# Issuing the four rough score products of the 8-dim attentions together, ahead of the weighing and the denominators

## The reference

```python
q = (x @ Wq + bq).reshape(B, N, 16, 8)
k = (y @ Wk + bk).reshape(B, M, 16, 8)       # y is x or the context
v = (y @ Wv + bv).reshape(B, M, 16, 8)
scores = einsum('bnhd,bmhd->bhnm', q, k) * scale   # + bias table in one, causal mask in another
attn = softmax(scores, axis=-1)
out = einsum('bhnm,bmhd->bnhd', attn, v).reshape(B, N, 128)
```

## Time and profile before

| what | us |
|---|---|
| median of 3 runs (3710.57 to 3713.22) | 3712.27 |
| the profiled execution, its own time | 3711.78 |
| its span from the first to the last instruction | 3710.0 |
| PE busy | 2897.6 (78%) |
| DVE busy | 2003.4 (54%) |
| ACT busy | 1416.0 (38%) |
| POOL busy | 1365.0 (37%) |
| TensorE's mean granted clock | 0.866 of full speed |

### The profile page before, as it was taken

How to read it: one execution, slowest core, us unless ns; L and a number is a source line. 1 busy time by engine, 2 the same in 40 slices (tenths; PEclk the granted TensorE clock), 3 DMA queues, 4 the chain that set the end, 5 groups by cost and what they waited for, 6 DMA issues and landing times. The chain is left out here.

```text
span 3710.0 us, 81900 instructions
## 1 busy us (share of the span) xinstructions
PE 2897.6 (78%) x32225; PEld 2044.2 (55%) x32225; DVE 2003.4 (54%) x5288; ACT 1416.0 (38%) x3283; POOL 1365.0 (37%) x1685
## 2 busy tenths in 40 slices
PE   6961566776686997996899869964589999979978
PEld 4540333554444775664799756641156666655657
DVE  6988887044463444663444445644455555535634
ACT  3541554144344553443222135520033333335544
POOL 3430343163201113544233334535533333325555
PEclk9985676577687998996999979967789999989979
DMA  2000000200000000000000000000000000000000
GB/s 92 3 2 2 1 1 1 79 21 1 6 1 30 2 2 36 3 3 1 7 1 1 1 13 2 2 38 0 0 5 2 2 2 2 2 7 2 2 1 23
DMA packets 24441, 36.96 MB, mean 10 GB/s; under 512 B 568, under 2 KB 21184, under 8 KB 23232
## 3 DMA queue, kind: packets, MB, share of 16 engines
q1 hardware_dynamic: 24096, 32.10, 2.7%
HBM read 29.87 MB, written 2.23 MB: 9 GB/s over the span
## 5 line engine op out<-in xcount | busy, mean ns | idle before, releaser
L1190 POOL TENSOR_TENSOR L_attn__qk<-L_attn__turned 128x512 f32<-128x512 f32 x128 | 161.5, 1273 | 381.0 <-DVE L_attn__turned L1299 381.0
L4079 PE MATMUL psum<-L_ffn_hT,weights 128*128 128x256 f32 x1024 | 244.9, 383 | 11.7 <-PEq L56 11.7
L1299 DVE TENSOR_TENSOR L_attn__turned<-psum,weights 128x1024 f32<-128x1024 f32 x128 | 153.7, 1221 | 153.1 <-PE psum L1406 149.9
L774 DVE TENSOR_REDUCE L_xattn__nm<-psum 128x8 bf16<-128x1024 f32 x128 | 156.4, 1225 | 147.2 <-PE psum L967 140.7
L4079 PEld LDWEIGHTS psum<-L_ffn_hT,weights 128*128 128x128 f32 x1024 | 186.8, 192 | 32.5 <-issue 11.8
L4018 DVE TENSOR_TENSOR L_ffn__e_a<-L_ffn__e_sg,psum 128x512 f32<-128x512 f32 x128 | 88.0, 688 | 187.4 <-ACT L_ffn__e_sg L4010 187.4
L4010 ACT ACTIVATE L_ffn__e_sg<-psum 128x512 f32<-128x512 f32 x128 | 76.4, 597 | 259.6 <-PE psum L4079 259.6
L714 ACT ACTIVATE L_xattn__pT<-psum 128x1024 f32<-128x1024 f32 x128 | 124.0, 1021 | 59.4 <-PE psum L995 59.4
L4090 PEld LDWEIGHTS psum<-weights,L_ffn__e_a 128*128 128x128 f32 x1024 | 134.4, 191 | 7.3 <-DVE L_ffn__e_a L4018 0.7
L1406 PE MATMUL psum<-L_attn__xT,weights 128*128 128x256 f32 x512 | 136.8, 401 | 1.7 <-DVE L_attn__turned L1299 1.0
L4090 PE MATMUL psum<-weights,L_ffn__e_a 128*128 128x128 f32 x1024 | 135.0, 275 | 0.5 <-DVE L_ffn__e_a L4018 0.5
(11 more groups left out here) (658 smaller groups left out, 8033.9 us busy)
## 6 DMA issues: line engine op xcount, KB each, us to landing
L_xattn__toeplitz<-s4d_kernel SPq DMA_DIRECT2D x8, 1024.0 KB, 5.6
weights<-pack SPq DMA_DIRECT2D x1, 3328.0 KB, 10.8
weights<-pack SPq DMA_DIRECT2D x1, 3140.0 KB, 11.4
weights<-pack SPq DMA_DIRECT2D x1, 2370.0 KB, 9.1
out_dram<-X SPq DMA_DIRECT2D x1, 2048.0 KB, 8.7
weights<-pack SPq DMA_DIRECT2D x1, 1732.5 KB, 10.3
ctxT<-ctxT_in SPq DMA_DIRECT2D x1, 1536.0 KB, 21.7
weights<-pack SPq DMA_DIRECT2D x1, 1376.0 KB, 5.8
```

Source lines behind the costliest of these rows:

```text
L774: nc.vector.tensor_reduce(nm[:, n % 2, :].rearrange("p (g c) -> p g c", g=4)[:, 2 * u:2 * u + 2, 0:4], scores[u].rearrange("p g (i q) -> p ...
L1190: nc.gpsimd.tensor_tensor(qk[:, p % 2, u], turned[:, g % 2, :, 0:2 * P], turned[:, g % 2, :, 2 * P:4 * P], ALU.add).then_inc(qk_sb, 1)
L1299: nc.vector.tensor_tensor(turned[:, g % 2], proj[u % 2].unsqueeze(1).to_broadcast([P, 2, 4 * P]), k.w(name + "rope").rearrange("p (t q) -> ...
L4079: last = nc.tensor.matmul(bank[g % 2][:, 256 * c:256 * c + 256], k.w(name + w)[:, o:o + P], hT, start=True, stop=True)
```

## The change

`score_roughly` takes no halves any more. It waits once, for `drained` at 2n (both halves of the block before read out), spreads bias or mask into all four banks in one run of sixteen 32x32 tiles, then issues the four score products one after another, one for each group of rows, and counts `rough_ps` up behind the second and the fourth. In the loop it stands whole ahead of `weigh`, which `add_up` now follows directly. The instructions are otherwise the same, in number, shape and data. `spread` takes a list of banks; where `score` calls it nothing changes.

```diff
-                def spread(u, addend):
+                def spread(banks, addend):
                     for j in range(4):
-                        for g in (2 * u, 2 * u + 1):
+                        for g in banks:
...
-                def score_roughly(n, halves):
+                def score_roughly(n):
                     b, s = n // 2 % 2, n % 2
                     pe.wait_ge(k16m_sb, n // 2 + 1)
                     pe.wait_ge(q16_sb, n // 2 + 1)
-                    for u in halves:
-                        if n >= 1:
-                            pe.wait_ge(drained, 2 * n - 1 + u)
-                        if bias:
-                            spread(u, bias16[:].rearrange("p (g h q) -> p g h q", g=4, h=4))
-                        if rope:
-                            spread(u, masks[:, 0])
-                        for g in (2 * u, 2 * u + 1):
-                            rows_g = slice(32 * g, 32 * g + 32)
...
-                        last.then_inc(rough_ps, 1)
+                    if n >= 1:
+                        pe.wait_ge(drained, 2 * n)
+                    if bias:
+                        spread(range(4), bias16[:].rearrange("p (g h q) -> p g h q", g=4, h=4))
+                    if rope:
+                        spread(range(4), masks[:, 0])
+                    for g in range(4):
+                        rows_g = slice(32 * g, 32 * g + 32)
...
+                        if g % 2 == 1:
+                            last.then_inc(rough_ps, 1)
...
                     if n + 1 < NB:
-                        score_roughly(n + 1, [0])
+                        score_roughly(n + 1)
                     if n >= 1:
                         weigh(n - 1)
-                    if n + 1 < NB:
-                        score_roughly(n + 1, [1])
-                    if n >= 1:
                         add_up(n - 1)
```

More of the change, by code:

```diff
@@ L957, in score_roughly @@
                     pe.wait_ge(q16_sb, n // 2 + 1)
-                    for u in halves:
-                        if n >= 1:
-                            pe.wait_ge(drained, 2 * n - 1 + u)
-                        if bias:
-                            spread(u, bias16[:].rearrange("p (g h q) -> p g h q", g=4, h=4))
-                        if rope:
-                            spread(u, masks[:, 0])
-                        for g in (2 * u, 2 * u + 1):
-                            rows_g = slice(32 * g, 32 * g + 32)
[L967 to L970, removed]
-                        last.then_inc(rough_ps, 1)
+                    if n >= 1:
[6 more added lines that the diff above has]
+                        rows_g = slice(32 * g, 32 * g + 32)
+                        last = nc.tensor.matmul(
+                            k.bank[4 + g], q16[rows_g, b, P * s:P * s + P],
+                            k16m[rows_g, b, s].rearrange("p i q -> p (i q)"),
+                            start=not (bias or rope), stop=True, skip_group_check=True)
+                        if g % 2 == 1:
+                            last.then_inc(rough_ps, 1)
                 def score(n, turned_before):
@@ L982, in score @@
                         if rope:
-                            spread(u, masks[:, 1])
+                            spread((2 * u, 2 * u + 1), masks[:, 1])
                     pe.wait_ge(qm_sb, n // 2 + 1)
@@ L1073, in _ @@
                     pe.wait_ge(bo_sb, 1)
-                score_roughly(0, (0, 1))
+                score_roughly(0)
                 if rope:
```

## The result

The changed kernel takes 3765.97 us in the median of four runs (3764.05 to 3767.88) where the kernel before, in its rounds, takes 3711.42: a ratio of 1.0148 with an interval of 1.0131 to 1.0166, about +55 us. A second comparison on another occasion gave 3762.87 against 3714.69, 1.0135 (1.0119 to 1.015). The forecast was 3752.7 us, +40.4, with a range of 3738 to 3778. The sign, the mechanism and the range held; the size was short by 8 to 14 us. In the rounds of the later runs single executions of the kernel before took 3704 to 3719 us, 0.4% from end to end, a wider scatter than the 0.1% of the first three. One of the eight executions of the last kernel of experiment 5 was slow, 4138.88 us at a mean granted clock of 0.685 where the others have 0.86, and is left out of its median.

What follows compares the result with a forecast made beforehand. It took the loop through the one set of score banks, not PE's busy time, as the bound: 16.8 + 9.0 - 1.8 + 16.4 = +40.4 us on 3712.27 gave 3752.7 us, range 3738 to 3778.

Steps and rivals of the forecast that it cites:

- rival (a): In the four stages PE is the bound after all: -72 us, 3640 us; chance 4%.
- the loop of exponentials, rough scores, maxima and exact scores: In the four stages a new block is once around the one set of score banks: +40.4 us in all.
- the signs that the prediction gave: PE busy about 80% in L3_xattn; in L0_attn a wait of about 1.6 us and a DVE gap of 0.9 us.
- What PE is spared: PE saves 0.43 us a block in the cross stages and 0.77 in L0_attn and L1_ffn.
- the lower bound that I had taken: In the spread, sixteen 32x32 tiles take the 0.34 us of eight; the upper end was 0.68.
- rival (c): Slower still on PE: tiles in two rounds, +20 us, or the clock falling in L0_attn, +15 us; chance 14%.
- The wait: The first rough product waits until both halves are read; in L3_xattn PE stands still for 0.83 us.
- The second wait, for DVE: In L3_xattn PE, through with rough scores, weighing and denominators after 2.23 us, waits about 0.6 us for DVE.
- The sum: Stage by stage: L3_xattn +16.8, L2_xattn +9.0, L1_ffn -1.8, L0_attn +16.4, in all +40.4 us.
- The term that was mis-sized: L0_attn, where DVE reads the banks: blocks of 7.22 and 7.65 us against 6.89, +0.55 a block, +16.4 us.
- (d): The loop as computed in the four stages: 3752.7 us, own range 3740 to 3765; chance 76%.

Runs made afterwards that it cites:

- the last kernel of experiment 5: Kernel before, with the second rough half in mid-weighing in L0_attn and L3_xattn, directly behind the first by one call in L1_ffn and L2_xattn: 3699.51 us, ratio 0.9966.
- Experiments 1 and 2: Kernel before, first rough half waiting for both halves: 3828.13 us; kernel before, both rough halves ahead of weighing, each with its own wait: 3709.39 us.
- experiment 3: Changed kernel, with L0_attn's output products issued three times over: 3759.39 us, ratio 1.0132; again, beside the changed kernel: 3760.91 us, 1.0129.

## Why the prediction held, and where it was short

*What bounds the stages.* The step from the busy shares to the loop was right. The earlier trace rows alone would have led to rival (a), 3640 us; the loop of exponentials, rough scores, maxima and exact scores is what closed the blocks. Experiments 1 and 2 show it from both sides, and the signs that the prediction gave came: PE busy for 81% of L3_xattn, the wait of 1.58 us in L0_attn, a gap of 0.95 us on DVE before the maxima there.

*What PE is spared.* Four products in 0.40 us were as the earlier trace rows had them. The sixteen tiles of 32x32, which no row had shown, take 0.44 us in the changed kernel where eight took 0.41, and 0.37 from start to start (139.64 to 140.01 above): the lower bound that I had taken, plus the 0.03 that the estimate by the Trainium skill ("TensorE: Matmul & The Clock Gate", Part 3 on packing small matmuls) added. The branch of rival (c) with two rounds is out.

*The wait.* 0.83 us was forecast for the idle PE in L3_xattn, and the loop had it: the row says 0.75, since a row's idle time counts from the modelled end of the matmul before. The second wait, for DVE, was given as about 0.6 us; the row shows 0.38, and the first transposition, 0.24, falls into the same time.

*The sum.* L3_xattn 6.48 for 6.50, L2_xattn 6.49 and 6.95 for 6.50 and 6.98, L1_ffn 7.20 for 7.16, L0_attn's undisturbed blocks 7.27 and 7.70 for 7.22 and 7.65. L1_ffn was given as -1.8 us and came to +0.8: its blocks are 0.04 us longer than computed, most of it the 0.03 of the sixteen tiles, and its last full block takes 8.70 us instead of 6.92. Without projections to fill the wait PE idles there for 2.10 us, and the two windows around it show the clock go:

```profile
1714.00:1718.00 4.00, 1.90 (x44) 0.75 (x44) 0.00 (x0) 1.94 (x2) 0.75 (x1) 1.00 0.00 0
1718.00:1722.00 4.00, 4.00 (x77) 3.18 (x73) 2.69 (x3) 0.20 (x1) 0.00 (x0) 0.58 0.02 4
```

*The term that was mis-sized is L0_attn's*, +16.4 us for a measured +27.3. The loop as such came to (7.27 + 7.70) / 2 - 6.89 = 0.60 us a block instead of 0.55, 18 us over 30 blocks. The other 9 us are the clock. I had kept it out of the sum and put it among the rivals, (c), at 1.0 us for each of 15 blocks and with 14% for both of its branches, though I had computed the idle stretch, 1.58 us, to the hundredth. It was not a rival to the loop but came on top of it: where the loop makes PE wait, the clock can fall. In the profile it fell in nine of the 15 blocks, at 0.7 to 1.0 us each, and in the last block, at 1.0. Filled idle time took 6.6 of these 9 us back (experiment 3); the blocks at the ends, which could not be filled, keep 2.5. The range held because it had been drawn to take in (c); the 3740 to 3765 us given for (d) alone were just left in the first comparison.

*What was not tried:* a kernel in which the joined products don't wait for both halves, since the banks would be overwritten while they are read; a second set of score banks would be needed, and PSUM has no room for one: the kernel's eight banks are the four of the scores and four in other use.

## What to carry to other kernels

A busy share of 95 to 100% doesn't prove that taking work off the engine pays: go once around the loop through the shared buffer with the durations of the rows, and see how far below the block's time it closes. Two halves of a buffer with a wait each are a pipeline; joining them to save a launch or to fill an array turns the waits of the later half into waits of everything. Where a change makes TensorE wait in a dense stage for as long as here (after gaps of 1.58 and 2.10 us the clock fell; in steady blocks with gaps of 0.75 and 1.01 it stayed), add the clock to the sum and not to the rivals; and where work has to go in between, move the second half to the moment when its banks come free.

## What the runs showed of the hardware

- Products on four row groups cost no more than on two (0.40 against 0.39 us for 512 columns), sixteen 32x32 tiles 0.03 us more than eight.
- Useless products can pay: 0.89 us of them in each second block held the granted clock at 1.00 where it had been 0.94, and shortened the stage by 6.6 us.
- The fall is not tied to each such gap. Of thirteen blocks with the same 1.58 us of idle PE five ran at full clock and took 7.27 us, eight fell and took 8.1 to 8.3.
